# Order of transfers, of GpSimd's steps and of the work on normalized rows in a chain of attention layers

## The chip, the cores and the metric

The kernel runs on one core of a Trainium2 chip. The metric is the time of one execution on the device, in microseconds (us), the median of three. The core has five engines that run side by side: TensorE (matrix products), VectorE, ScalarE, GpSimd, and SyncE, which only issues transfers. Each takes its instructions in order; semaphores tie them together.

## The reference, cut to what matters

Eight batches of 512 tokens with 256 features go through eight stages. Five are attention with 16 heads of 16 features, two are two-layer networks, and the last is attention with heads of 64.

```
stage    kind
SELF0    x += attend(q, k, v of norm(x), causal) . W + b
CROSS0   x += attend(q of norm(x), k, v of ctx) . W + b
MLP0     x += gelu(norm(x) . W1 + b1) . W2 + b2
CROSS1   x += attend(q of norm(x), k, v of ctx) . W + b, weights quantized to -1, 0, 1 times a scale
SELF2    x += attend(q, k, v of norm(x), mask added) . W + b
CROSS2   as CROSS0
MLP2     as MLP0
SELF3    x += attend(q of norm(x), k, v of norm(ctx), causal) . W + b, heads of 64

attend:  scores = q . k^T * scale; softmax over keys (with the maximum of each query taken off); . v
```

## The kernel before

An attention stage is worked off in units: half a batch's heads, 8 heads x 512 queries x 512 keys, so 16 units of a stage (`UNITS`). Each engine runs the same sequence of slots, one for each unit, from `run_slots(engine, s, slot)`; `U` counts units over all stages, `u` those of a stage, `half` is `u % 2`. A stage whose predecessor is attention too is joined to it without a gap. In slot `u` TensorE works on three units at once:

- for unit u + 1, 32 tiles of maxima (`max_tile`: queries x keys, 128 queries x 512 keys, into the banks MX; VectorE reduces each to one maximum for a query),
- for unit u, 32 tiles of scores, turned (`score_tile`: keys x queries, into the banks ST; ScalarE takes the exponential into `prob`), and their products with the values (`values`, into OUT),
- for unit u + 2, the projections to keys and queries, and for each whole batch the values, the turning of the normalized rows (`T0`, `T1`) and the output projection (`O0`, `O1`). All of these pass through one bank L, one after the other: at which run of tiles each stands is written in the table `AT`, and `L_NO` numbers the uses of the bank. ScalarE or VectorE empties it and counts `l_free`; TensorE waits for that before the next use.

The maxima of a unit are needed as rows beside the stacked queries and keys. GpSimd splits them into a high and a low part (`split_max`), TensorE turns them (`M0` for the heads of group 0, `M1` for group 1), ScalarE copies them to `mrows` (`rows_out`), and SyncE copies two rows to `stk` (`max_rows`). Queries and keys are rounded to a high part `hi` and a remainder `lo` by GpSimd (`split`), and each of the two kinds (0 keys, 1 queries) is put into `stk` by three copies of 128 KB for each group of heads (`stack`), so that one matrix product holds all parts. At the first tile of a slot and at its 17th, TensorE waits for both kinds of stacked rows of that group of the next unit (`stack_in`) and for the rows of maxima of its own (`mrow_in`).

The other tasks of SyncE's queue in a slot: `move_few` and `move_raw` take the sums of exponentials and the raw products to other partitions, `spread_rows` and `widen` send the inverted sums through memory and back, `load_ctx` fetches a batch of the context. SyncE waits in order: whatever stands behind a wait waits too.

GpSimd multiplies the raw products by the inverted sums once for each unit (the operation at L1911, the scaling), and counts `at_ready`, for which the output projection O0 of an even slot waits. In CROSS1, whose weights are exact in the reduced format, the scaled products are also split in two parts (`output_parts`), and so are the normalized rows `hT` for the queries (`normed_parts`: `hT_hi`, then `hT_lo`), 14 times in attention slots; the first batch is done ahead of the stage. ScalarE writes `hT` out of bank L (`normalized`).

Of the kernel before, what the change touches and what calls it, by code (L numbers as in the profile page):

```python
# [73 lines left out]
def program(nc, x_in, ctx_in, ctx_rows_in, masks_in, shapes_in, cols_in, rows_in, wts, out):  # L74
# [12 lines left out]
    with es:  # L87
# [282 lines left out]
        def a_of(s, u, b):  # L370

            return (s + 1, b + 1 - NB) if isinstance(u, int) and u >= UNITS - 2 else (s, b + 1)
# [24 lines left out]
        def turn_of(s, u):  # L397

            if u == -2:
                return (s, 0) if s == SELF0 else None  # L400
            if u % 2 and (u + 1 < UNITS - 2 or s + 1 in JOINED and u < UNITS):
                return a_of(s, u + 1, (u + 1) // 2)
            return None
# [5 lines left out]
        L_NO = {}  # L409
# [118 lines left out]
        def _(sp):  # L528
# [25 lines left out]
            def attention(s):  # L554
                cross, causal, addmask = ATTN[s]
                n = ATTN_NO[s]

                def slot(u, c, b, p, on):
                    half, U, GB = c % 2, UNITS * n + u, NB * n + b
                    if u == 2:  # L560
                        load_next(s)
                    if (s, u) == (CROSS1, UNITS - 1):
                        sp.wait_ge(l_full, L_NO[s, u - 1, "O1"] + 1)
                        sp.dma_start(mask_k, masks_in[:, NT:2 * NT, :]).then_inc(masks_loaded, 16)
                    if on["stack1"]:
                        stack(U + 1, 1 - half, 1, 0)
                    if on["tail"]:
                        move_few(U - 1, 1 - half, 1)
                        move_raw(U - 1, 1 - half, 1, GB - 1 + half)
                    if on["b"]:  # L570
                        max_rows(U, half, 1)
                    if on["stack1"]:
                        stack(U + 1, 1 - half, 1, 1)
                    if on["tail"]:
                        spread_rows(U - 1, 1 - half)
                        widen(U - 1, 1 - half)
                    if cross and half == 0 and 0 <= b < NB - 2:
                        sp.wait_ge(l_full, L_NO[(*kq_slot(U + 1), "V1")] + 1)
                        load_ctx(b + 2, c // 2)
                    if on["a"]:  # L580
                        for kind in range(2):
                            stack(U + 2, half, 0, kind)
                    if on["b"]:
                        move_few(U, half, 0)
                    if on["m"]:
                        max_rows(U + 1, 1 - half, 0)
                    if on["b"]:
                        move_raw(U, half, 0, GB)

                def stack(U, half, g, kind):  # L590

                    if kind == 0:
                        wait(sp, st_full, 32 * (U - 2) + 16 * (g + 1))
                    sp.wait_ge(lo_done, 2 * U + kind + 1)
                    at = (8 if kind == 0 else 0) + G * g
                    for r, part in enumerate(((hi, lo, hi), (hi, hi, lo))[kind]):
                        lo_p = 64 * half + HD * r
                        sp.dma_start(stk[lo_p:lo_p + HD, at:at + G, :].bitcast(F32),
                                     part[64 * g:64 * g + 64, kind, :].bitcast(F32)).then_inc(stack_in[g][kind], 16)

                def max_rows(U, half, g):
                    sp.wait_ge(l_free, max_job(U, g) + 1)
                    lo_p = 64 * half + 3 * HD
                    sp.dma_start(stk[lo_p:lo_p + 2, G * g:G * g + G, :].bitcast(F32),
                                 mrows[32 * g:32 * g + 2 * G, :]).then_inc(mrow_in[g], 16)

                def move_few(U, half, g):

                    waits(sp, (ov_evac, 2 * U + g + 1),
                          (spread_out, 16 * (U - 1)))  # L610
                    sp.dma_start(few[64 * g:64 * g + 64, half, :], ovs[1:P:32, g, :].rearrange("h (c n) -> h c n", n=32)).then_inc(few_in[g], 16)

                def move_raw(U, half, g, GBu):

                    wait(sp, at_ready, BASE + U - 1)
                    if GBu > 0:
                        sp.wait_ge(l_full, out_job(GBu - 1) + 1)
                    sp.dma_start(raw[64 * g:64 * g + 64, half, :], ovs[0:P:2, g, :]).then_inc(raw_in[g], 16)

                def spread_rows(U, half):  # L620

                    sp.wait_ge(recip_done, U + 1)
                    sp.dma_start(spread[half].rearrange("h (c n) -> (h c) n", n=32), few[:, half, :]).then_inc(spread_out, 16)

                def widen(U, half):
                    waits(sp, (spread_out, 16 * (U + 1)), (at_ready, BASE + U))
                    rows = spread[half].rearrange("h (a n) -> h a n", a=1).broadcast_to([2 * G, HD, S])
                    sp.dma_start(sums[:, half, :], rows).then_inc(spread_in, 16)

                if cross and s not in JOINED:  # L630
                    load_ctx(1, 1)

                def with_stack1(u, c, b, p, on):
                    slot(u, c, b, p, dict(on, stack1=on["m"]))

                run_slots(sp, s, with_stack1)
# [544 lines left out]
        def _(act):  # L1181
# [5 lines left out]
            def attention(s):  # L1187
# [3 lines left out]
                def slot(u, c, b, p, on):  # L1191
                    half, U = c % 2, UNITS * n + u
                    sa, _ = a_of(s, u, b)
                    if u == -2 and not turned_ahead(s, u):
                        normalized(sa, u, 0)
                    if turned_ahead(s, u):
                        high_part(sa, u, U, half, 1)
                    place = AT[addmask]
                    for r, run in enumerate(RUNS[addmask]):
# [10 lines left out]
                        if on["b"] and r == FIRST_OUT[addmask]:  # L1210
                            product_out(U, 0)
                        if half == 0 and on["a"] and r == place["T1"] and not turned_ahead(s, u):
                            normalized(sa, u, 1)
                        if on["b"] and r == place["M1"]:
                            rows_out(u, U, 1)
                        if on["a"] and r in (place["K1"], place["Q"]) and not (turned_ahead(s, u) and r == place["Q"]):
# [1 line left out]
                        if on["m"] and r == place["M0"]:  # L1218
                            rows_out(u, U + 1, 0)
                        if half == 1 and r == place["T0"] and turn_of(s, u) is not None:  # L1220
                            normalized(turn_of(s, u)[0], u, 0)
                        for part in range(2):
                            if to_mlp(s, u, UNITS - 1) and r == place[f"K{part}"]:
                                first_turned(u, U, part)

                def normalized(sa, u, c):

                    job = L_NO[s, u, ("T0", "T1")[c]]
                    act.wait_ge(l_full, job + 1)
                    nc.scalar.activation(hT[:, c, :], L[:, :], ACT.Identity, **scale_shift(sa, c)).then_inc(l_free, 1)  # L1230

                def first_turned(u, U, c):
# [185 lines left out]
        def _(dve):  # L1418
# [34 lines left out]
            def invert(U, half):  # L1453
# [2 lines left out]
                    dve.wait_ge(few_in[g], 16 * U)  # L1456
                nc.vector.reciprocal(few[:, half, :], few[:, half, :]).then_inc(recip_done, 1)

            def low_normed(c):
                nc.vector.tensor_tensor(lo[:, c, :], hT[:, c, :], hi[:, c, :].bitcast(F32), ALU.subtract).then_inc(ml_lo, 1)  # L1460

            def attention(s):
# [3 lines left out]
                def slot(u, c, b, p, on):  # L1466
# [13 lines left out]
                    for r, run in enumerate(RUNS[addmask]):  # L1480
                        for k in run:
                            if on["m"] and k % 16 == 0:
                                wait(dve, max_split, 2 * (U + 1) - 3 + k // 16)
                            if on["m"]:
                                max_tile(m_of(s, u), U + 1, 1 - half, k)
                            if on["b"] and addmask and k % G in BY_VECTOR:
                                add_mask(u, U, k)
                        if u != -2 and norm is not None and r < 2:
                            sn, bn = norm
                            if r == 0 and (s, u) == (SELF0, -1):  # L1490
                                dve.wait_ge(x_loaded, 16)
                            if r == 0 and sn > 0:
                                wait(dve, x_done, NB * (sn - 1) + bn + 1)
                            for t in (2 * r, 2 * r + 1):
                                statistics(NB * sn + bn, xt(bn, t), t)
# [285 lines left out]
        def _(pool):  # L1781
# [56 lines left out]
            def attention(s):  # L1838
# [12 lines left out]
                def slot(u, c, b, p, on):  # L1851
# [10 lines left out]
                        clear(U - 1, 7)  # L1862
                    if on["b"]:
                        maxima(U, half, 1)
                    if s == CROSS1 and u >= 0 and half == 0 and on["a"] and a_of(s, u, b)[0] == s:
                        for kind, job in enumerate((L_NO[s, u - 1, "T0"], L_NO[s, u, "T1"])):
                            pool.wait_ge(l_free, job + 1)
                            normed_parts(b + 1, kind)
                    if clears:
                        clear(U, 0)  # L1870
                    if adds:
# [31 lines left out]
                        clear(U, 4)  # L1903
                    if adds:
                        add_mask(u, U, 4)
                    if on["tail"]:
                        for g in range(2):
                            pool.wait_ge(raw_in[g], 16 * U)
# [3 lines left out]
                                                ALU.mult).then_inc(raw_scaled if into_parts else at_ready, 1)  # L1912
                        if into_parts:
                            output_parts(UNITS - 1 if u == 0 else u - 1)
                    if on["a"]:
                        split(u, U, half, 1)
                    if clears:
                        clear(U, 5)
                    if adds:
# [268 lines left out]
```

## Time and profile before

| | |
|---|---|
| median of 3 runs | 3846.8 us |
| lowest and highest | 3839.29 and 3864.33 us |
| profiled execution | 3851.18 us |
| its span, first to last instruction | 3849.1 us |
| granted TensorE clock, mean | 0.963 of 2.4 GHz |
| busy: TensorE, VectorE, ScalarE, GpSimd | 3607.1, 2775.6, 2455.8, 2132.5 us |

Busy times are sums over stages of different kinds, so the stretches of the single stages say more than they do. The attention stages with heads of 16 take these stretches of the span: SELF0 about 66 to 500 us, CROSS0 to 922, CROSS1 1210 to 1653, SELF2 to 2220, CROSS2 to 2646. A slot lasts 25 to 30 us in SELF0, 28 in CROSS0 and CROSS2, 27 in CROSS1 and 33 to 38 in SELF2.

### The profile page before, as it was taken

The page shows a single profiled execution, that of the slowest core. Times are in us where ns is not written, and L with a number is a line of the kernel's source. Part 1 is how long each engine was busy: PE and PEld are TensorE (multiplying, and loading weights), DVE is VectorE, ACT ScalarE, POOL GpSimd, SP SyncE. Part 2 cuts the span into 40 slices and gives each one's busy share as a digit, 9 for nine tenths or more (in the row PEclk, how much of TensorE's full clock was granted, in tenths as well). Part 3 has the DMA queues.
Part 4 walks back from the last instruction along what each step waited for, and adds up shares of the span by engine and source line. Part 5 has one row for each costly group of instructions (what it writes and reads, how often), then busy time and mean ns, then how long its engine had stood idle before and what let it go on. Part 6 is the DMA issues. An engine that isn't in the chain of part 4 may idle for free.

```text
span 3849.1 us, 69127 instructions
## 1 busy us (share of the span) xinstructions
PE 3607.1 (94%) x21778; PEld 2053.1 (53%) x21778; DVE 2775.6 (72%) x6841; ACT 2455.8 (64%) x5254; POOL 2132.5 (55%) x2103
## 2 busy tenths in 40 slices
PE   6999999999998999999999999999899999999998
PEld 3444444444884444333333344444787777776776
DVE  4566677776676788789999878776766666666664
ACT  2555567777333777778888877776236666666664
POOL 3465544332344555378988843422436767776765
PEclk8999999999997999989999999998899999999998
DMA  4433344432003534333222243431100000000000
GB/s 109 100 83 81 85 107 86 86 84 50 20 1 67 112 86 95 86 74 76 60 61 67 59 107 85 91 83 41 46 6 6 12 12 7 12 12 7 12 7 6
DMA packets 135374, 220.50 MB, mean 57 GB/s; under 512 B 42721, under 2 KB 44641, under 8 KB 133217
## 3 DMA queue, kind: packets, MB, share of 16 engines
q1 hardware_dynamic: 135008, 216.02, 25.0%
q8 instruction: 182, 2.98, 0.4%
q14 instruction: 184, 1.50, 0.2%
HBM read 59.69 MB, written 5.51 MB: 17 GB/s over the span
## 4 chain that ended last, share of the span: by engine, by line
PE 58%; DVE 16%; POOL 11%; ACT 5%; issue 5%; DMA 3%; SPq 1%; DVEq 0%; POOLq 0%; ACTq 0%
PE MX L703 17%; PE L L703 14%; PE OUT L703 12%; PE ST L703 11%; DVE mx L1523 4%; POOL prob L1968 3%; DVE h_lo L1566 2%; DVE h_hi L1564 2%; POOL prob L2040 2%; ACT prob L1262 2%; DVE MX L1516 1%; PE L L928 1%; PE MX L1069 1%; POOL lo L1958 1%; DMA stk<-mrows 1%
## 5 line engine op out<-in xcount | busy, mean ns | idle before, releaser
L1262 ACT ACTIVATE prob<-ST 128x512 f32<-128x512 f32 (+3 forms) x2304 | 1149.8, 572 | 428.2 <-PE ST L703 423.2
L1523 DVE TENSOR_REDUCE mx<-MX 128x1 f32<-128x512 f32 x1536 | 961.8, 682 | 199.0 <-PE MX L703 198.2
L703 PE MATMUL MX<-stk 48*128 48x512 f32 (+3 forms) x2560 | 913.6, 444 | 92.8 <-DMA stk<-lo 27.8
L703 PE MATMUL ST<-stk 50*128 50x512 f32 (+3 forms) x2560 | 934.4, 446 | 5.6 <-ACT prob L1262 4.2
L703 PEld LDWEIGHTS MX<-stk 48*128 48x128 f32 x2560 | 424.4, 191 | 678.5 <-DVE mx L1523 277.8
L2040 POOL TENSOR_SCALAR prob<-prob,mx 128x128 f32<-128x128 f32 (+3 forms) x512 | 557.2, 1101 | 278.9 <-DVE mx L1714 278.9
L703 PE MATMUL OUT<-prob,V 128*32 128x512 f32 (+3 forms) x5120 | 667.9, 595 | 10.7 <-ACT prob L1272 6.0
L703 PEld LDWEIGHTS ST<-stk 50*128 50x128 f32 x2560 | 428.0, 189 | 56.6 <-ACT prob L1262 23.5
L1516 DVE CUSTOM_DVE_ANT_0 MX<-MX,W_even 128x512 f32<-128x512 f32 x512 | 347.2, 700 | 40.0 <-PE MX L703 39.7
L1968 POOL TENSOR_TENSOR prob<-prob,W_odd 128x512 f32<-128x512 f32 x256 | 324.0, 1282 | 76.0 <-ACT prob L1262 75.5
L1520 DVE CUSTOM_DVE_ANT_0 MX<-MX,later 128x128 f32<-128x128 f32 (+3 forms) x512 | 237.2, 518 | 129.3 <-PE MX L703 128.4
L1272 ACT ACTIVATE prob<-prob 128x512 f32<-128x512 f32 x512 | 304.9, 624 | 12.1 <-POOL prob L1968 11.7
L1811 POOL TENSOR_TENSOR X<-X,brow 128x1024 f32<-128x1024 f32 x56 | 135.9, 2426 | 249.8 <-DVE X L1442 249.8
L1722 DVE COPY PT<-MX 128x128 f32<-128x128 f32 (+3 forms) x256 | 124.9, 488 | 196.3 <-PE MX L1069 196.3
L1355 ACT ACTIVATE prob<-MX,mx 128x128 f32<-128x128 f32 (+3 forms) x256 | 135.3, 528 | 136.2 <-DVE mx L1708 134.5
L703 PEld LDWEIGHTS OUT<-prob,V 128*32 128x32 f32 x5120 | 102.1, 109 | 220.5 <-issue 194.1
L1956 POOL CAST hi<-Pr 128x512 fp32r<-128x512 f32 x160 | 97.6, 610 | 219.2 <-ACT Pr L1249 199.2
L1958 POOL TENSOR_TENSOR lo<-Pr,hi 128x512 fp32r<-128x512 f32 x160 | 204.5, 1278 | 12.9
L1302 ACT ACTIVATE V<-MX,cols 128x512 f32<-128x512 f32 x64 | 44.0, 690 | 231.5 <-PE MX L703 231.5
L1975 POOL TENSOR_SCALAR_AFFINE_SELECT prob<-prob 128x512 f32<-128x512 f32 x128 | 81.3, 635 | 185.0 <-ACT prob L1262 185.0
L1532 DVE TENSOR_TENSOR prob<-ST,W_odd 128x512 f32<-128x512 f32 x256 | 175.2, 684 | 0.0
L1249 ACT ACTIVATE Pr<-L,cols 128x512 f32<-128x512 f32 x128 | 88.0, 688 | 136.4 <-PE L L703 133.7
(238 smaller groups left out, 7527.8 us busy)
## 6 DMA issues: line engine op xcount, KB each, us to landing
stk<-hi SPq DMA_DIRECT2D x640, 128.0 KB, 3.8
stk<-lo SPq DMA_DIRECT2D x320, 128.0 KB, 3.9
misc<-misc SPq DMA_DIRECT2D x160, 128.0 KB, 2.8
sums<-spread SPq DMA_DIRECT2D x80, 256.0 KB
ctx_full<-in_ctx_t SPq DMA_DIRECT2D x24, 512.0 KB, 6.9
W_even<-in_w SPq DMA_DIRECT2D x2, 2048.0 KB, 11.3
XH<-in_ctx_rows SPq DMA_DIRECT2D x8, 512.0 KB, 3.6
X<-in_x_t SPq DMA_DIRECT2D x1, 3584.0 KB, 14.7
```

The costliest lines, as they stand in the source:

```text
L703: return nc.tensor.matmul(o, l, r, start=start, stop=stop)
L1262: nc.scalar.activation(prob_at(k)[:, q0:S], STB[k % RING][:, q0:S], ACT.Copy if addmask else ACT.Exp).then_inc(ex_done, 2 if addmask else 1)
L1272: nc.scalar.activation(tile, tile, ACT.Exp).then_inc(late_done, 1)
L1355: nc.scalar.activation(P3(qt, h)[:, 0:k_n], S3[h][t % 2][:, 0:k_n], ACT.Exp, bias=low3[:, qt, h:h + 1], scale=-1.0, accum_out=total3[:, qt ...
L1516: nc.vector.tensor_tensor_reduce(bank[:, :], bank[:, :], mask_q[:, qt, :], 1.0, -3.0e38, ALU.add, ALU.max, m).then_inc(mx_red, 1)
L1520: nc.vector.tensor_tensor_reduce(bank[:, 0:k_n], bank[:, 0:k_n], later0[:, S - k_n:S], 1.0, -3.0e38, ALU.add, ALU.max, m).then_inc(mx_red, 1)
L1523: nc.vector.tensor_reduce(m, bank[:, :], AX.X, ALU.max).then_inc(mx_red, 1)
L1532: nc.vector.tensor_tensor(prob_at(k), STB[k % RING], mask_k[:, i % 4, :], ALU.add).then_inc(st_masked, 1)
L1811: nc.gpsimd.tensor_tensor(xt(b, 0, NT), xt(b, 0, NT), bias, ALU.add).then_inc(x_done, 1)
L1958: nc.gpsimd.tensor_tensor(lo[:, kind, :], kq[:, kind, :], hi[:, kind, :].bitcast(F32), ALU.subtract).then_inc(lo_done, 1)
L1968: nc.gpsimd.tensor_tensor(tile, tile, mask_k[:, i % 4, :], ALU.add).then_inc(pool_masked, 1)
L2040: nc.gpsimd.tensor_scalar(tile, tile, inv3[:, qt, h:h + 1], None, ALU.mult).then_inc(nm3_done, 1)
```

## The change

In every attention stage, SyncE's copy of the rows of maxima for group 0 goes between the stacked keys and the stacked queries of that group, ahead of the queries and of `move_few`. In every attention stage, GpSimd splits the queries (kind 1) ahead of the scaling. In CROSS1, for all batches but the first, ScalarE writes the high part `hT_hi` itself, out of bank L and ahead of `hT`, and VectorE subtracts to get `hT_lo` in the second and third run of tiles of an even slot; GpSimd's `normed_parts` is left out there.

```diff
@@ SyncE, slot
                     if on["a"]:
-                        for kind in range(2):
-                            stack(U + 2, half, 0, kind)
+                        stack(U + 2, half, 0, 0)
+                    if on["m"]:
+                        max_rows(U + 1, 1 - half, 0)
+                    if on["a"]:
+                        stack(U + 2, half, 0, 1)
                     if on["b"]:
                         move_few(U, half, 0)
-                    if on["m"]:
-                        max_rows(U + 1, 1 - half, 0)
                     if on["b"]:
                         move_raw(U, half, 0, GB)
@@ ScalarE
-                def normalized(sa, u, c):
+                def normalized(sa, ba, u, c):
                     job = L_NO[s, u, ("T0", "T1")[c]]
                     act.wait_ge(l_full, job + 1)
+                    if sa == CROSS1:
+                        nc.scalar.activation(hT_hi[ba == 0][:, c, :], L[:, :], ACT.Identity, **scale_shift(sa, c)).then_inc(h_high, 1)
                     nc.scalar.activation(hT[:, c, :], L[:, :], ACT.Identity, **scale_shift(sa, c)).then_inc(l_free, 1)
@@ VectorE
+            def low_part(ba, c):
+                nc.vector.tensor_tensor(hT_lo[:, c, :], hT[:, c, :], hT_hi[ba == 0][:, c, :].bitcast(F32),
+                                        ALU.subtract).then_inc(h_low, 1)
...
+                        if half == 0 and u >= 0 and on["a"] and sa == CROSS1 and r in (1, 2):
+                            dve.wait_ge(l_free, L_NO[(s, u - 1, "T0") if r == 1 else (s, u, "T1")] + 1)
+                            low_part(b + 1, r - 1)
@@ GpSimd, slot
                     if on["b"]:
                         maxima(U, half, 1)
-                    if s == CROSS1 and u >= 0 and half == 0 and on["a"] and a_of(s, u, b)[0] == s:
-                        for kind, job in enumerate((L_NO[s, u - 1, "T0"], L_NO[s, u, "T1"])):
-                            pool.wait_ge(l_free, job + 1)
-                            normed_parts(b + 1, kind)
...
                     if adds:
                         add_mask(u, U, 4)
+                    if on["a"]:
+                        split(u, U, half, 1)
                     if on["tail"]:
                         for g in range(2):
                             pool.wait_ge(raw_in[g], 16 * U)
...
                             output_parts(UNITS - 1 if u == 0 else u - 1)
-                    if on["a"]:
-                        split(u, U, half, 1)
                     if clears:
                         clear(U, 5)
```

## Rows read from the trace of the kernel before

**Rows 1.** Windows: SELF0, CROSS0, CROSS1, SELF2: length, busy, clock, DMA share, GB/s

```profile
65.80:499.90 434.10, 411.58 (x2613) 205.60 (x2612) 283.37 (x1104) 248.78 (x623) 236.12 (x316) 0.95 0.39 85
499.90:922.50 422.60, 413.06 (x2530) 181.83 (x2529) 331.76 (x581) 305.47 (x582) 155.79 (x181) 1.00 0.42 89
1210.00:1653.00 443.00, 415.82 (x2601) 178.15 (x2600) 356.95 (x654) 332.61 (x624) 223.54 (x253) 0.98 0.42 92
1653.00:2220.30 567.30, 520.42 (x2631) 217.38 (x2629) 518.94 (x1361) 468.22 (x877) 481.29 (x448) 0.93 0.29 66
```

**Rows 2.** Waits of TensorE, total us, times, longest: CROSS1, then CROSS0

```profile
PE MX L703 <- DMA stk<-mrows: 18.4, 12, 2.5
...
PE MX L703 <- DVE mx L1523: 4.2, 17, 0.7
```

**Rows 3.** SyncE's queue in time, two slots of CROSS0: start us, us

```profile
704.86 0.70 SPq L604 DMA_DIRECT2D stk<-mrows  x1
...
706.86 0.60 SPq L598 DMA_DIRECT2D stk<-lo  x1
...
720.20 0.60 SPq L598 DMA_DIRECT2D stk<-lo  x1
...
722.75 0.68 SPq L604 DMA_DIRECT2D stk<-mrows  x1
```

**Rows 4.** ScalarE's rows and TensorE's next slot start: CROSS0 twice, SELF0, CROSS1 twice

```profile
722.14 0.59 ACT L1277 ACTIVATE mrows<-L 8x512 f32<-8x512 f32 x1 [0.32 <-PE L L928]
727.80 0.50 PE L703 MATMUL MX<-stk 48*128 48x512 f32 x1
...
692.77 0.59 ACT L1277 ACTIVATE mrows<-L 8x512 f32<-8x512 f32 x1 [0.69 <-PE L L928]
700.06 0.50 PE L703 MATMUL MX<-stk 48*128 48x512 f32 x1
...
334.58 0.59 ACT L1277 ACTIVATE mrows<-L 8x512 f32<-8x512 f32 x1 [0.82 <-PE L L928]
339.63 0.29 PE L703 MATMUL MX<-stk 48*128 48x128 f32 x1
...
1449.91 0.59 ACT L1277 ACTIVATE mrows<-L 8x512 f32<-8x512 f32 x1 [0.65 <-PE L L928]
1457.01 0.46 PE L703 MATMUL MX<-stk 48*128 48x512 f32 x1 [1.30 <-DMA stk<-mrows]
...
1232.31 0.59 ACT L1277 ACTIVATE mrows<-L 8x512 f32<-8x512 f32 x1 [0.65 <-PE L L928]
1235.75 0.49 PE L703 MATMUL MX<-stk 48*128 48x512 f32 x1
```

**Rows 5.** Transfers: KB, us from issue to landing; chain: landing to TensorE's start

```profile
stk<-lo SPq DMA_DIRECT2D x320, 128.0 KB, 3.9
...
570.93 0.09 issue
```

**Rows 6.** SELF2: GpSimd in time, TensorE, its waits for GpSimd, VectorE

```profile
1890.11 1.29 POOL L1911 TENSOR_TENSOR misc<-misc,sums 128x512 f32<-128x512 f32 x1
...
1892.03 1.27 POOL L1958 TENSOR_TENSOR lo<-Pr,hi 128x512 fp32r<-128x512 f32 x1
...
1891.45 0.48 PE L703 MATMUL L<-W_even,misc 128*128 128x256 f32 x1 [0.45 <-POOL misc L1911]
...
PE L L703 <- POOL misc L1911: 3.2, 7, 0.6
PE L L703 <- POOL raw_lo L1945: 2.5, 1, 2.5
...
1893.48 0.69 DVE L1442 TENSOR_TENSOR X<-L,X 128x512 f32<-128x512 f32 x1 [0.51 <-PE L L703]
```

**Rows 7.** CROSS1, an even slot in time: ScalarE, TensorE, GpSimd

```profile
1432.41 0.78 ACT L1230 ACTIVATE hT<-L,cols 128x512 f32<-128x512 f32 x1
...
1433.24 0.27 PE L928 MATMUL L<-ident,mhl 128*8 128x128 f32 x1
...
1440.42 0.61 POOL L1956 CAST hi<-Pr 128x512 fp32r<-128x512 f32 x1 [5.21 <-ACT Pr L1249]
```

More of the change, by code:

```diff
@@ L1194, in slot @@
                     if u == -2 and not turned_ahead(s, u):
-                        normalized(sa, u, 0)
+                        normalized(sa, 0, u, 0)
                     if turned_ahead(s, u):
@@ L1212, in slot @@
                         if half == 0 and on["a"] and r == place["T1"] and not turned_ahead(s, u):
-                            normalized(sa, u, 1)
+                            normalized(*a_of(s, u, b), u, 1)
                         if on["b"] and r == place["M1"]:
@@ L1220, in slot @@
                         if half == 1 and r == place["T0"] and turn_of(s, u) is not None:
-                            normalized(turn_of(s, u)[0], u, 0)
+                            normalized(*turn_of(s, u), u, 0)
                         for part in range(2):
```

## The prediction

> **What bounds the kernel now.** I call one of the 16 half-batches of an attention stage a slot; in a slot TensorE does 32 tiles of maxima of the next unit and 32 of scores of its own. I read the windows first, one for each attention stage [rows 1]. TensorE is busy 413 of 423 us in CROSS0, 416 of 443 in CROSS1, 412 of 434 in SELF0 and 520 of 567 in SELF2, while VectorE has 332, 357, 283 and 519. So TensorE's own queue sets the time, and a wait that ends in it is paid in full; in SELF2 VectorE is as tight, and no slack is left there either. Then I read who waits for whom on TensorE [rows 2]. In CROSS1 it waits 12 times, 18.4 us in all, for the rows of maxima to land: that is what the change is after. In CROSS0 no such wait is in the list at all; the list's longest is 4.2 us for VectorE.
>
> **Where the slot starts.** TensorE starts a slot when three things have landed for heads of group 0: stacked keys, stacked queries, and the rows of maxima. The last two are what the change swaps in SyncE's queue. In CROSS0 the queries went out long before (third copy issued at 720.20) and the queue then stood idle until ScalarE had the rows of maxima; it sent them at 722.75, at once [rows 3]. ScalarE finished them at 722.14 + 0.59 = 722.73, and TensorE went on at 727.80 without a wait [rows 4]: 5.07 us later. That is the time in which anything issued behind the rows has to land. After an even slot it is 700.06 - 693.36 = 6.70 us; in SELF0 before an even slot 339.63 - 335.17 = 4.46 us; in CROSS1 1457.01 - 1450.50 = 6.51 us, of which 1.30 are the wait [rows 4].
>
> **The swap in SyncE's queue.** After the change the three copies of queries stand behind the rows of maxima, and the rows wait for ScalarE. The same order is already used for the heads of group 1, so its price is in the trace: from the issue of rows of maxima to that of the third copy behind it 706.86 - 704.86 = 2.00 us [rows 3]. The third copy lands 3.9 us after its issue (the median of 320) [rows 5], and TensorE starts 0.09 us after a landing [rows 5]. With 0.02 from ScalarE's end to the issue, a slot can't start before ScalarE's end + 0.02 + 2.00 + 3.9 + 0.1 = 6.0 us. Against the distances above:
> CROSS0, starts of even slots: 6.0 - 5.07 = 0.95 us late, 7 of them (u = 2 to 14), 6.6 us. CROSS2 has the same code and the same work: 6.6 us. Starts of odd slots have 6.70 and lose nothing.
> SELF0, even: 6.0 - 4.46 = 1.55 us, 7 of them: 10.9 us.
> CROSS1 in its middle: the start moves from 6.5 (odd) to 6.0; before even slots the gain is some 0.2. About 12 starts, on average 0.35 us each: 4 us saved. This is all that is left of the 18.4 us, since the queries take the place of the rows as what lands last.
> CROSS1, u = 1: ScalarE ends at 1232.90 and TensorE starts at 1235.75 without a wait [rows 4], 2.85 us; it will be 6.0, so 3.1 us.
> The other first and last starts of the stages, some eight with distances between the ones shown: 0 to 12 us, I take 8 (about 1 each, as in CROSS0).
> SELF2: ScalarE has the rows ready far ahead there, the queries are last in either order; 0.
> The swap costs 6.6 + 6.6 + 10.9 - 4 + 3.1 + 8 = 31 us. The copies of sums of exponentials and of raw products move behind the queries too; they are read in the next slot, and cost nothing as long as the queue is empty by then: the rows and five more issues of 0.6 us each are out some 3.9 us after ScalarE's end, ahead of the slot's start.
> What is not shown is whether the three copies land as fast here as elsewhere: between 3.9 us alone for one copy after 2.00 us of issues, and nothing at all, if their first packets ran beside the rows. The row is of the same copies in the same order, so I take it.
>
> A rule of the Trainium skill speaks for less. The page "DMA: Bandwidth & Descriptors", section "Anatomy of one DMA — SWDGE (gpsimd) path", gives a copy about 2.0 us plus its bytes by 436 GB/s; 128 KB would be an estimated 2.3 us, and the queries would land 4.4 us after ScalarE's end, inside all distances but that of u = 1. The section is about copies that GpSimd issues, these are SyncE's, and the traced 3.9 us decides.
>
> **GpSimd's order.** The splitting of the queries (0.6 and 1.3 us) moves ahead of the scaling of the product. In the trace the scaling ends at 1891.39 and the splitting at 1893.30 [rows 6], so the scaling ends 1.91 us later from now on, and the queries 1.3 us earlier (3.2 in CROSS1, where the scaling also makes two parts). Earlier queries help nothing where SyncE holds them behind the rows. Later scaling costs where the output projection waits for it. That is SELF2: TensorE starts the projection at 1891.45, the moment the scaling is done, after 0.45 us of waiting; the stage has 7 such waits, and one more for the parts of CROSS1's last batch [rows 6]. So 8 x 1.91 = 15.3 us. VectorE, which could have hidden it, idles at the same place already, 0.51 us for that projection [rows 6], and finds no other work in its order. In CROSS0 and CROSS1 TensorE's list has no wait for the scaling [rows 2], and I take 0 there; with a margin of less than 1.9 us it would be up to 1 us for each of 16 projections. If TensorE caught up behind VectorE, SELF2 would pay 5 us; more than 15.3 has no mechanism.
>
> **Parts of rows in CROSS1.** GpSimd loses 14 pairs of operations, ScalarE gains 14 of 0.78 us and VectorE 14 of some 0.69. GpSimd stood idle 5.2 us before its splitting of keys [rows 7], so it didn't bound anything. ScalarE's new one stands between the transposed rows and the release of their bank, and TensorE's turning of the maxima needs that bank: it begins at 1433.24, just as ScalarE ends 1432.41 + 0.78 = 1433.19 [rows 7]. Every even slot moves by 0.75 us there, 7 of them: 5.2 us. The second bank of each batch is released at the end of an odd slot, a run of tiles ahead of its next use: 0. VectorE's 0.69 us fall into a stage where it is busy 357 of 443 us [rows 1], and are hidden by a ring of three banks; bounds 0 and 14 x 0.69 = 10 us.
> Here the Trainium skill has a warning: by "SBUF — State Buffer", section "Who interferes with whom", a VectorE operation with two inputs in SBUF and a GpSimd operation that reads SBUF lock each other out. GpSimd has no work at that point of the slot once its parts are gone, so the estimate by the rule is 0, and at worst one GpSimd operation of 1.3 us for each of the 14; no row here shows the two beside each other.
>
> **TensorE's clock.** It was granted fully in CROSS0 (1.00) and at 0.98 in CROSS1, which has the waits, 0.95 in SELF0 and 0.93 in SELF2 [rows 1]; these are means over stretches at 2.4 and at 1.2 GHz, so that 0.02 less is 2% of the time. If CROSS0 and CROSS2 fell to CROSS1's level, twice 423 us x 0.02 = 17 us; if the other two lost as much, 20 more. Below: 0. Rows of a stage with waits of this size are nearer to the small end, and I take 6.
>
> **Sum.** 31 + 15.3 + 5.2 + 6 = 58 us. The profiled execution took 3851.2 us (span 3849.1), 4.4 above the median of three, 3846.8. So 3909 on its own scale and 3905 on the median's: 1.5% slower.
>
> **Rivals.**
> (a) Not slower. The queries never land last: the decisive number is the time from ScalarE's end to their landing, 6.0 by my rows; at 4.4 or below no start but that of u = 1 is late, and CROSS1's 18.4 us are gained whole. For it: the trace shows no query copy in that place for group 0. Against it: the same three copies behind the same rows, group 1. 3847 - 18 + 15 + 5 = 3849; with SELF2's price gone as well, 3834. Chance 0.17, of which 0.05 is faster by over 1%: only with clock given back too.
> The estimate from the Trainium skill's "DMA: Bandwidth & Descriptors" would put the landing at those 4.4 us; the trace doesn't bear it out for any copy of this size.
> (b) SELF2 hides the later scaling, because TensorE is ahead of VectorE's maxima in most of the stage (it waits for them at slot starts). Against it is VectorE's own idle time at that place. 3905 - 10 to 15 = 3892. Chance 0.15.
> (c) The start waits are partly made good inside the slot, so that half of the 31 are paid: 3889. For it: TensorE's busy time is not its peak. Chance 0.10.
> (d) The clock falls in the wake of the new waits, most of the 37 us above: 3935 to 3950. For it: the two stages with most waits have the lowest clock. Chance 0.10.
> The forecast itself: 0.48.
>
> A measurement of this kernel tells about 1% from no change (the three runs spread over 0.65%), so slower means above 3885. The forecast, (b), (c) and (d) lie mostly above it, but (c) and part of (b) with a small clock term lie close: slower 0.70, same 0.25, faster 0.05. For 8 in 10 the range goes down into the upper part of (a), 3856, and up into (d), 3940.
>
> **What the new profile would show.** Right: TensorE's waits for maxima rows gone from CROSS1 and waits for the third query copy in their place, about 1 us at even starts of CROSS0 and CROSS2 and 1.5 in SELF0, ScalarE's end to slot start at 6.0; in SELF2 the wait for the scaling at 2.4 instead of 0.45; in CROSS1 a wait of 0.7 before the turned maxima. Wrong: slots of CROSS0 as long as before (the landing is shorter), or SELF2's slots as long (hidden). What would break the sum: another landing time of the copies, or clock stretches that move by tens of us.

## The result

The changed kernel takes 3927.0 us (median of 4, 3909.95 to 3945.51) against 3853.2 us for the kernel before (median of 4, 3839.29 to 3864.33). The ratio is 1.0194, with a 95% interval of 1.0133 to 1.0256: slower by some 74 us. The profiled execution took 3920.8 us, 69.6 more than that of before, and its span is 3919.0 us.

### The profile after

First the windows of the changed kernel, one for each attention stage: SELF0, CROSS0, CROSS1, SELF2, CROSS2. The columns are those of [rows 1]: length, then busy time and instructions of TensorE, its weight loads, VectorE, ScalarE and GpSimd, then the granted clock, the DMA share and GB/s.

```profile
68.70:525.40 456.70, 427.47 (x2614) 209.81 (x2614) 283.37 (x1102) 250.75 (x623) 236.23 (x316) 0.90 0.38 81
525.40:959.80 434.40, 415.89 (x2528) 181.75 (x2528) 331.67 (x580) 305.86 (x581) 156.01 (x178) 0.99 0.41 86
1248.20:1696.60 448.40, 417.49 (x2602) 179.95 (x2602) 365.43 (x668) 341.65 (x638) 197.40 (x224) 0.97 0.43 92
1696.60:2284.20 587.60, 526.12 (x2629) 219.97 (x2629) 520.27 (x1361) 468.92 (x877) 481.59 (x445) 0.92 0.29 64
2284.20:2719.70 435.50, 418.66 (x2535) 182.22 (x2535) 332.05 (x581) 309.16 (x586) 157.69 (x182) 0.99 0.41 86
```

CROSS2 in the kernel before, which [rows 1] leaves out:

```profile
2220.30:2646.00 425.70, 418.13 (x2536) 183.29 (x2536) 332.39 (x581) 308.18 (x586) 156.79 (x182) 0.99 0.41 88
```

TensorE has the same instructions in both kernels (the counts of a stage differ by two at most). So each stage's loss can be split in two: what its busy time grew by is time in which it ran slower, at the clock's lower level; what is left of the length (length less busy) is time in which it stood. From these windows and [rows 1]:

| stage | length | TensorE busy | TensorE standing |
|---|---|---|---|
| SELF0 | +22.6 | +15.9 | +6.7 |
| CROSS0 | +11.8 | +2.8 | +9.0 |
| CROSS1 | +5.4 | +1.7 | +3.7 |
| SELF2 | +20.3 | +5.7 | +14.6 |
| CROSS2 | +9.8 | +0.5 | +9.3 |
| sum | +69.9 | +26.6 | +43.3 |

The spans differ by the same 69.9 us (3919.0 - 3849.1): outside these stages the differences cancel (2.9 us more ahead of SELF0, 0.9 more between CROSS0 and CROSS1, 3.8 less behind CROSS2). Each kernel's column is one execution, and the clock differs from one execution to the next. How much the busy column can be trusted is seen in the traces of the experiments below. SELF0 was busy 401.0 to 416.8 us in seven traces without the swap there, and 427.5, 436.6 and 438.2 in the three with it, so its growth is real. SELF2 was busy 516.4 to 531.1 us in four traces in which the code of the stage was unchanged, so its +5.7 says nothing.

**What TensorE waits for.** TensorE's list of waits in CROSS0, then CROSS1, then SELF2 (total us, times, longest):

```profile
PE MX L704 <- issue: 8.4, 8, 1.6
...
PE MX L704 <- DMA stk<-lo: 3.0, 2, 2.0
```

```profile
PE MX L704 <- issue: 17.3, 15, 2.0
PE MX L704 <- DMA stk<-lo: 6.5, 3, 3.5
PE L L929 <- ACT hT L1233: 3.4, 6, 0.6
```

```profile
PE L L929 <- POOL mhl L1846: 21.0, 16, 2.8
PE L L704 <- POOL misc L1920: 16.5, 7, 2.4
...
PE L L704 <- POOL raw_lo L1952: 4.4, 1, 4.4
```

"Issue" says that the profile matched no releaser. The wait for `stk<-mrows` of [rows 2] is gone from CROSS1, but waits of these two kinds stand at the same starts: the twelve that took 18.4 us now take 15.4, and u = 1, which had none, waits 3.5. CROSS0 had two waits of these kinds, 2.1 us in all, and has ten. What ended them is seen by following one start of CROSS0 through three engines in time (start us, length us): ScalarE, SyncE's queue, TensorE.

```profile
753.46 0.59 ACT L1280 ACTIVATE mrows<-L 8x512 f32<-8x512 f32 x1 [0.32 <-PE L L929]
...
754.07 0.69 SPq L605 DMA_DIRECT2D stk<-mrows  x1
754.80 1.19 SPq L599 DMA_DIRECT2D stk<-hi  x2
756.04 0.60 SPq L599 DMA_DIRECT2D stk<-lo  x1
...
760.20 0.46 PE L704 MATMUL MX<-stk 48*128 48x512 f32 x1 [1.03 <-issue]
```

ScalarE ends at 754.05; the rows go out at once, the third copy of the queries at 756.04, 1.97 us behind; TensorE starts at 760.20. That is 6.15 us after ScalarE's end, where the distance was 5.07 before [rows 3, 4]. The third copy explains it: the median of all 320 from issue to landing is 3.9 us in this trace too, as in [rows 5], and 0.02 + 1.97 + 3.9 is 5.9 of the 6.15. The other even starts agree: 6.14 to 6.20 us from u = 2 to 12 in CROSS0 and 6.59 at u = 14; in SELF0 6.13 to 6.16 at five of the seven, 6.63 and 6.42 at the other two.

In SELF2 GpSimd now finishes the scaling at 1944.82 + 1.27 = 1946.09, behind the splitting; TensorE starts the projection at 1946.15, and VectorE, which had idled 0.51 us for it [rows 6], idles 2.42:

```profile
1943.59 1.28 POOL L1965 TENSOR_TENSOR lo<-Pr,hi 128x512 fp32r<-128x512 f32 x1
1944.82 1.27 POOL L1920 TENSOR_TENSOR misc<-misc,sums 128x512 f32<-128x512 f32 x1
...
1946.15 1.99 PE L704 MATMUL L<-W_even,misc 128*128 128x256 f32 x8 [2.35 <-POOL misc L1920]
...
1948.18 0.69 DVE L1445 TENSOR_TENSOR X<-L,X 128x512 f32<-128x512 f32 x1 [2.42 <-PE L L704]
```

**Where the clock fell.** One even start of SELF0 in the changed kernel: TensorE's first product, then windows of 6.7 us from there (TensorE's busy time comes first behind the length, the granted clock third from the end).

```profile
353.27 0.29 PE L704 MATMUL MX<-stk 48*128 48x128 f32 x1 [1.67 <-issue]
```

```profile
353.30:360.00 6.70, 6.70 (x38) 3.69 (x42) 3.44 (x15) 5.50 (x11) 0.64 (x1) 0.53 0.40 60
360.00:366.70 6.70, 6.70 (x32) 1.96 (x24) 2.68 (x12) 1.72 (x6) 1.27 (x2) 0.71 0.30 61
```

The same place of the kernel before, whose slot starts at 339.63 without a wait [rows 4]:

```profile
339.60:346.30 6.70, 5.98 (x45) 3.14 (x44) 4.37 (x20) 6.37 (x13) 1.47 (x5) 1.00 0.37 82
346.30:353.00 6.70, 6.67 (x41) 2.63 (x40) 4.50 (x19) 3.48 (x10) 2.34 (x5) 1.00 0.36 75
```

After a wait of 1.67 us TensorE runs the next ones at 0.53 and 0.71 of 2.4 GHz, which is mostly its lower level of 1.2 GHz; without the wait it keeps 1.00 there. In the changed kernel such a stretch of 7 to 10 us begins within 0.6 us of the start at all seven even slots u = 2 to 14 of SELF0, in the kernel before at none of them. Over the whole stage the clock's record has 92 us at the lower level in the changed kernel and 41 in the kernel before. So the theory for what the forecast undersized was: the swap's waits are as computed, and they cost the clock as well. The rival was that waits or transfers somewhere else had grown.

### The profile page after: what moved, and what is told of

Read it like the earlier page. It is cut to its first block, busy times and chain, and to the rows that moved or that the text cites. A ratio compares the mean times of both kernels' runs of the same rounds, so it can differ in the third digit from the quotient of the medians.

```text
span 3919.0 us, 69127 instructions
## 1 busy us (share of the span) xinstructions
PE 3629.8 (93%) x21778; PEld 2057.2 (52%) x21778; DVE 2782.2 (71%) x6855; ACT 2472.7 (63%) x5268; POOL 2110.7 (54%) x2075
## 4 chain that ended last, share of the span: by engine, by line
PE 61%; DVE 14%; POOL 11%; issue 6%; ACT 5%; DMA 2%; SPq 1%; DVEq 0%; POOLq 0%; ACTq 0%
PE MX L704 17%; PE L L704 15%; PE OUT L704 13%; PE ST L704 11%; DVE mx L1534 4%; POOL prob L1975 3%; DVE h_lo L1577 2%; DVE h_hi L1575 2%; POOL prob L2047 2%; DMA stk<-lo 2%; PE L L929 1%; PE L L727 1%; ACT prob L1265 1%; PE MX L1070 1%; DVE st L1426 1%
## 5 line engine op out<-in xcount | busy, mean ns | idle before, releaser
L704 PE MATMUL OUT<-prob,V 128*32 128x512 f32 (+3 forms) x5120 | 678.7, 604 | 7.8 <-POOL prob L1982 4.1
L1844 POOL CAST mhl<-mx 128x16 fp32r<-128x16 f32 x160 | 33.2, 207 | 263.7 <-DVE mx L1534 247.9
```

Source lines behind the costliest of these rows:

```text
L704: return nc.tensor.matmul(o, l, r, start=start, stop=stop)
```

## The experiments

Every time stands beside runs of the kernel before on the same chip; ratios are to those, with 95% intervals.

### The three parts alone

The swap in SyncE's queue alone, all stages:

```diff
                     if on["a"]:
-                        for kind in range(2):
-                            stack(U + 2, half, 0, kind)
-                    if on["b"]:
-                        move_few(U, half, 0)
+                        stack(U + 2, half, 0, 0)
                     if on["m"]:
                         max_rows(U + 1, 1 - half, 0)
+                    if on["a"]:
+                        stack(U + 2, half, 0, 1)
+                    if on["b"]:
+                        move_few(U, half, 0)
```

> The swap in SyncE's queue alone. Queue theory (queries that go out behind the rows of maxima land last, 6.1 us after ScalarE's end): 31 us slower by the prediction's sum, up to 40 with clock, most of it in SELF0, CROSS0 and CROSS2, about 1 us at each start of an even slot there; CROSS1 within 5 us of before. Rival (clock: the loss is in stretches at 1.2 GHz and not in the waits): well under 31 us, with CROSS0 as long as before.

Measured: 3918.9 us, ratio 1.0173 (1.0136 to 1.0209), some 67 us. The windows of SELF0, CROSS0 and CROSS2:

```profile
69.80:534.80 465.00, 436.59 (x2614) 213.52 (x2614) 283.76 (x1102) 252.37 (x624) 236.85 (x318) 0.88 0.38 80
534.80:969.50 434.70, 417.32 (x2528) 181.97 (x2528) 331.72 (x580) 305.83 (x581) 155.57 (x178) 0.99 0.41 86
...
2278.10:2718.40 440.30, 421.16 (x2535) 182.92 (x2535) 332.12 (x581) 309.93 (x589) 158.70 (x183) 0.98 0.41 85
```

Standing grew by 5.9, 7.8 and 11.6 us in these and by 3.2 in CROSS1 (30.4 for 27.2): 28.5 us, where I had computed 31. In SELF2 it didn't grow. Busy time grew by 25.0 us in SELF0 alone, by 4.3, 3.3 and 3.0 in CROSS0, CROSS1 and CROSS2, and fell by 2.7 in SELF2: 33 us in all. The other 11.7 us by which this span is longer than that of before (3922.3 for 3849.1) lie outside these stages, and no experiment shows why. So the waits were sized right and the clock was not: up to 40 us were expected and 67 measured. The swap is nearly the whole loss, and nearly half of its profiled loss is growth of busy time.

GpSimd's order alone, all stages:

```diff
+                    if on["a"]:
+                        split(u, U, half, 1)
                     if on["tail"]:
...
                             output_parts(UNITS - 1 if u == 0 else u - 1)
-                    if on["a"]:
-                        split(u, U, half, 1)
```

> GpSimd's order alone, in all stages. Own theory: SELF2 longer by 15 us (8 waits for the scaling, 1.9 us each more), CROSS1 shorter by up to 18 us, since the queries' copies leave 3 us earlier and the rows of maxima no longer queue behind them; the sum within 5 us of before. Rival (the order is free because VectorE bounds SELF2): 18 us faster than before.

Measured: 3853.6 us, 0.9984 (0.9959 to 1.0009): no change that can be measured. But it is two opposite effects, CROSS1 and SELF2 in the windows:

```profile
1221.90:1640.90 419.00, 410.70 (x2601) 177.95 (x2600) 356.56 (x654) 331.58 (x624) 223.97 (x253) 0.99 0.49 98
1640.90:2232.60 591.70, 531.13 (x2631) 221.03 (x2630) 522.40 (x1361) 469.94 (x877) 482.37 (x448) 0.90 0.28 63
```

CROSS1 is 24 us shorter than in [rows 1], SELF2 24 us longer.

The parts of rows by ScalarE and VectorE alone (the edits to `normalized`, `low_part` and `normed_parts` of the diff ahead of the prediction, with both orders as before):

> The parts of rows by ScalarE and VectorE alone. Own theory: a new wait of 0.5 to 0.75 us ahead of the turned maxima in 7 even slots of CROSS1, 0 to 5 us slower, partly absorbed by the wait for the rows of maxima that is still there. Rival (freeing GpSimd is what brings the gain): CROSS1 shorter by 5 us or more.

Measured: 3862.6 us, 1.0013 (0.9991 to 1.0034). In CROSS1 TensorE's waits for ScalarE ahead of the turned maxima are there, and the waits for rows of maxima of [rows 2] stay:

```profile
PE MX L703 <- DMA stk<-mrows: 19.1, 12, 2.5
PE L L928 <- ACT hT L1232: 4.4, 7, 0.6
```

4.4 us for the computed 5.2: right. The stage's standing grew by 4.1 us (31.3 for 27.2).

### GpSimd's order, stage by stage

The same edit with the condition `s == CROSS1`, and with `s == SELF2`:

```diff
+                    if on["a"] and (s == CROSS1):
+                        split(u, U, half, 1)
                     if on["tail"]:
...
-                    if on["a"]:
+                    if on["a"] and not (s == CROSS1):
                         split(u, U, half, 1)
```

> GpSimd's order in CROSS1 only, everything else as before. Own theory: all of the 12 waits for rows of maxima go and nothing takes their place, because the queries leave some 3 us before the rows are ready: 18 us faster, 0.5%. Rival (another wait ends at the same place, as with the swap): within 5 us of before.

> GpSimd's order in SELF2 only. Own theory: 8 waits for the scaling 1.9 us longer each, 15 us slower, plus some us of lower clock (24 us more in SELF2 with the order in all stages). Rival (VectorE's backlog hides them): within 5 us of before.

Measured: in CROSS1 alone 3830.6 us, 0.9942 (0.9923 to 0.9961), 22 us faster than the kernel before and by its ratio the fastest of all versions. In SELF2 alone 3882.8 us, 1.0054 (1.0034 to 1.0074), 21 us slower: in its trace the stage is 29.6 us longer (596.9), with 15.7 us more standing, where 15.3 were computed, and 13.9 more busy time, some of which the unchanged stage shows in other traces too. The two cancel, as the run with both shows.

Why CROSS1 gains is seen in SyncE's queue. GpSimd in the kernel before (scaling, its parts, then the queries' parts), and the queue:

```profile
1445.88 1.27 POOL L1911 TENSOR_TENSOR misc<-misc,sums 128x512 f32<-128x512 f32 x1 [2.77 <-DMA sums<-spread]
...
1449.83 1.28 POOL L1958 TENSOR_TENSOR lo<-Pr,hi 128x512 fp32r<-128x512 f32 x1
...
1443.94 8.39 SPq L598 DMA_DIRECT2D stk<-hi  x3
1452.37 0.60 SPq L598 DMA_DIRECT2D stk<-lo  x1
...
1453.71 0.68 SPq L604 DMA_DIRECT2D stk<-mrows  x1
```

The rows were ready at 1450.50 [rows 4] and went out at 1453.71: they stood behind the queries' copies, these waited for GpSimd, and GpSimd had stood 2.77 us for the inverted sums. With the queries' parts first:

```profile
1447.11 1.28 POOL L1960 TENSOR_TENSOR lo<-Pr,hi 128x512 fp32r<-128x512 f32 x1
1448.36 1.27 POOL L1913 TENSOR_TENSOR misc<-misc,sums 128x512 f32<-128x512 f32 x1
...
1449.65 0.60 SPq L598 DMA_DIRECT2D stk<-lo  x1
...
1451.88 0.59 ACT L1277 ACTIVATE mrows<-L 8x512 f32<-8x512 f32 x1 [0.64 <-PE L L928]
...
1452.49 0.68 SPq L604 DMA_DIRECT2D stk<-mrows  x1
...
1457.61 0.50 PE L703 MATMUL MX<-stk 48*128 48x512 f32 x1
```

The queue is empty when ScalarE ends (1452.47), the rows go out at 1452.49, and TensorE starts 5.14 us after ScalarE's end instead of 6.51, without a wait. No wait for the rows is left in this stage, and it is 20.8 us shorter than before (422.2 for 443.0), 18.3 of them standing. In the change itself the swap puts the queries behind the rows and takes this gain away again.

For SELF2 the gain to be had would be to move the scaling ahead instead. I took the fastest version and let GpSimd do the scaling between its two additions of the mask in even slots:

```diff
+                    early = adds and half == 0
                     if adds:
-                        add_mask(u, U, 4)
+                        add_mask(u, U, 4, BY_POOL[:1] if early else BY_POOL)
...
+                        if early:
+                            add_mask(u, U, 4, BY_POOL[1:])
```

> GpSimd's order in CROSS1 only, and the opposite move in SELF2: in even slots the scaling goes 1.3 us earlier, between the two mask additions ahead of it. Own theory (TensorE's wait for the scaling is paid in full): those waits, 5.7 us in all before, go, and SELF2 is some 5 us shorter; in all 20 to 25 us faster than before. Rival (the later mask addition holds up its exponential instead): no faster than the order in CROSS1 alone, with TensorE's waits for ScalarE's exponentials longer.

Measured: 3836.7 us, 0.9949 (0.993 to 0.9968): 20 us faster than the kernel before, but not faster than the order in CROSS1 alone. The wait for the scaling is gone from SELF2's list. TensorE stands 40.8 us there, instead of 43.4 with the order in CROSS1 alone and 46.9 in the kernel before, but it is busy 531.7 us instead of 521.9 and 520.4, at a clock of 0.90:

```profile
1647.10:2219.60 572.50, 531.73 (x2630) 219.89 (x2629) 519.86 (x1361) 470.70 (x877) 481.34 (x447) 0.90 0.29 66
```

What was saved in waits didn't show in the time. The rival's reason isn't seen: TensorE's waits for exponentials ahead of its products with the values are 2.1 us, against 2.0 with the order in CROSS1 alone. Whether the edit itself lowers the clock isn't settled: with the code of this stage unchanged it lasted from 562.9 to 573.7 us over the experiments.

### The swap, stage by stage

In SyncE's slot `ahead = s == CROSS0`, and the rows go ahead of the queries where `ahead` is true, else as before; then the same with `s == SELF0`.

```diff
+                    ahead = s == CROSS0
...
+                        stack(U + 2, half, 0, 0)
+                    if on["m"] and ahead:
+                        max_rows(U + 1, 1 - half, 0)
+                    if on["a"]:
+                        stack(U + 2, half, 0, 1)
...
-                    if on["m"]:
+                    if on["m"] and not ahead:
```

> The swap in CROSS0 only. Own theory: starts of even slots 1.0 to 1.1 us later, 8 of them, 9 to 12 us slower in all, without more than 10 us at the lower clock, since the waits there are shorter. Rival (the clock follows any such wait): 20 us slower.

> The swap in SyncE's queue in SELF0 only. Wait theory (the swap costs the waits it makes): 12 to 15 us slower. Clock theory (each wait of some 1.6 us at the start of an even slot is followed by 7 to 10 us at 1.2 GHz, as in both traces with the swap): SELF0 25 us or more longer, with 50 us more at the lower clock than before.

Measured: CROSS0 alone 3868.9 us, 1.0024 (1.0008 to 1.004), some 9 us; SELF0 alone 3893.2 us, 1.0083 (1.0055 to 1.011), some 32 us. Seven even starts, late by about 1 us each, cost CROSS0 what the waits are: TensorE's standing there grew by 9.4 us and its busy time by 5.4. In SELF0 waits of 1.7 us at the starts cost three times my 10.9, and the clock's record has 116 us at the lower level for the 41 of before, as the clock theory wanted. Its windows, whole and after an even start:

```profile
68.60:535.60 467.00, 438.21 (x2614) 213.49 (x2614) 283.12 (x1102) 251.25 (x623) 235.99 (x316) 0.88 0.38 79
...
359.90:366.60 6.70, 6.70 (x38) 3.75 (x42) 3.40 (x15) 5.46 (x11) 0.63 (x1) 0.53 0.40 60
```

To see whether the low clock comes from standing, I filled these waits: the swap in SELF0, and TensorE works off twelve 128 x 128 products with the identity ahead of its wait in even slots. They write a bank that the first tile overwrites.

```diff
+                            if k == 0 and on["m"] and s == SELF0 and half == 0:
+                                wait(pe, mx_red, TILES * U + before(0) + 1)
+                                for _ in range(12):
+                                    mm(MXB[0][:, 0:P], identr[:, :], identr[:, :])
```

> The same swap in SELF0, and TensorE does 12 small products of the identity (about 1.3 us, written to a bank that the next tile overwrites) ahead of its wait at the start of each even slot of SELF0. They compute nothing that is used. The queries still land 6.1 us after ScalarE's end, so the slot can't start sooner. Clock theory: no long stretches at 1.2 GHz after these starts, 8 to 15 us faster than with the swap in SELF0 alone. Wait theory: the same time as that, or slower if the products take longer than the wait.

Measured: 3886.7 us, 1.0069 (1.0049 to 1.009): 6 us less than unfilled, but the intervals overlap. The same start, and the windows after it:

```profile
357.73 1.53 PE L707 MATMUL MX<-identr 128*128 128x128 f32 x12
359.64 0.29 PE L707 MATMUL MX<-stk 48*128 48x128 f32 x1 [0.37 <-issue]
```

```profile
359.60:366.30 6.70, 5.97 (x44) 3.05 (x44) 4.16 (x18) 5.71 (x12) 1.16 (x2) 1.00 0.39 59
366.30:373.00 6.70, 6.53 (x40) 2.63 (x40) 4.50 (x19) 3.49 (x10) 2.34 (x5) 1.00 0.35 74
```

The start is as late as without them, 6.15 us after ScalarE's end in both, and the clock stays at 1.00 in these two windows. So it is with all the filled starts of the stage: no low stretch begins there. Standing, not lateness, brings the low stretch. Low stretches elsewhere in the stage stay (72 us in all, against 116 unfilled and 41 before); one begins 14 to 18 us after each of the seven starts.

Over the stage TensorE's busy time without the fillers (10.8 us) falls from 438.2 to 431.8 - 10.8 = 421.0 us. Of these 17.2 us only 7.9 are gained in the stage (467.0 to 459.1), because other waits come back: those for `hT`, 5.2 us before and none in the swapped kernels, are 4.8 us again, and one for VectorE takes 2.7. A slower TensorE had been hiding those for `hT`. So in this stage the clock's cost is less than the growth of busy time. In the whole time the filled kernel's gain is too small for these runs, and the two profiled executions (3897.5 and 3900.4 us) don't show it at all.

### The parts together

GpSimd's order in all stages and the parts of rows, without the swap; and the fastest version with the parts of rows added:

> The changed kernel with SyncE's queue as it was before: GpSimd's order in all stages and the parts of rows. Own theory: the swap is what costs; CROSS1 some 15 us shorter than before, SELF2 15 to 25 us longer, within 15 us of the kernel before in all and 55 us or more faster than the changed kernel. Rival (the three parts need each other, and the loss comes from order or parts): still 30 us or more slower than before.

> GpSimd's order in CROSS1 only, with the parts of rows by ScalarE and VectorE. Own theory: the waits for rows of maxima are gone already with the order, so the parts only add 3 to 5 us of waits ahead of the turned maxima: 13 to 15 us faster than before, 3 to 5 us slower than with the order alone. Rival (GpSimd's free time helps once the rows don't wait): 5 us or more faster than the order alone.

Measured: all but the swap 3866.8 us, 1.0032 (1.0015 to 1.005), so the swap costs 1.0194 / 1.0032 = 1.016 on top of the rest, as it does alone. The rival is out, but one step of the expectation is too: CROSS1 lasted 439.5 us, 3.5 shorter than before and not 15, at 424.9 busy and a clock of 0.96. The order in CROSS1 with the parts of rows 3850.5 us, 0.9991 (0.997 to 1.0011): 0.0049, 19 us, slower than the order alone, where some 5 us of waits were expected. The wait, and the window of CROSS1 in this kernel:

```profile
PE L L928 <- ACT hT L1232: 8.5, 7, 1.3
```

```profile
1200.20:1638.90 438.70, 424.02 (x2603) 181.19 (x2602) 365.59 (x668) 340.69 (x638) 197.31 (x225) 0.96 0.46 93
```

and the window of CROSS1 with the order alone:

```profile
1221.20:1643.40 422.20, 413.29 (x2601) 178.35 (x2600) 356.58 (x654) 331.64 (x624) 223.56 (x253) 0.98 0.48 97
```

Once the start waits are gone, the wait for ScalarE grows from 0.6 to 1.2 us each. ScalarE used to catch up while TensorE stood at the start. Now it is late: TensorE has filled the bank at 1309.70 + 0.66 = 1310.36, and ScalarE begins on it 0.80 us later, behind three exponentials and a copy of the products:

```profile
1309.70 0.66 PE L726 MATMUL L<-ident,XH 128*128 128x128 f32 x4
...
1311.16 0.81 ACT L1231 ACTIVATE hT_hi_later<-L,cols 128x512 fp32r<-128x512 f32 x1
```

With the parts alone it began 0.03 us after, at a start with a wait of 1.16 us (1383.27 for 1383.24). Standing grows by 14.7 - 8.9 = 5.8 us, busy time by 10.7: again more busy time is added than standing. The low stretches stand where the new wait is: one of 3.4 to 6.8 us begins within 1.5 us of five of the six waits of 1.33 us. The kernel with all but the swap shows it at five of six too, within 2.3 us. This makes the parts of rows dear just where the order made the stage fast.

## Why the prediction was right, and where its terms were not

The forecast was 3905 us, 1.015 of its median before; the interval of the measured ratio, 1.0194 (1.0133 to 1.0256), includes that. The waits came where they were said to come and at nearly their size. One term, the clock's, was far too small, and the total is closer than its terms because the waits were put somewhat too high: that part is luck.

**Slot start at ScalarE's end + 6.0.** Right, a little short: 6.15 in CROSS0, 353.27 - (346.52 + 0.59) = 6.16 in SELF0, where ScalarE's row is

```profile
346.52 0.59 ACT L1280 ACTIVATE mrows<-L 8x512 f32<-8x512 f32 x1 [0.81 <-PE L L929]
```

The row of the same copies in another place of the slot was a good price. Rival (a), the queries never last, is out. The estimate of 2.3 us for 128 KB by the rule of the Trainium skill's "DMA: Bandwidth & Descriptors", section "Anatomy of one DMA — SWDGE (gpsimd) path", doesn't hold for these copies: from SyncE's queue they took 3.9 us. The rule is for copies that GpSimd issues, and no run here tests it on those. The nearest copy of this size in SyncE's queue, `misc<-misc`, had a median of 2.8 us in the trace of before, so the landing time goes by the kind of copy too, and the row of the same copies was the one to take.

**The swap's waits, 31 us.** 28.5 in the swap alone, as growth of TensorE's standing. In CROSS1 the twelve waits fell by 3.0 us for the computed 4, and u = 1 waits 3.5 for 3.1. CROSS0 and CROSS2 took 9.0 and 9.3 in the changed kernel for 6.6 and their edges. SELF0 took 6.7 net for 10.9 and its edges, since its waits for `hT` vanished meanwhile.

**SELF2, 15.3 us.** 14.6 of standing, 15.7 with the order in SELF2 alone. Waits for the scaling grew from 3.2 to 16.5 and from 2.5 to 4.4 us. Rival (b), hidden in part, is out; TensorE's wait for the maxima's parts even grew from 17.0 to 21.0 us, which I hadn't computed, while its waits for VectorE fell.

**Parts of rows, 5.2 us.** 3.4 in the changed kernel (6 waits of 0.6), 4.4 alone. The rule of the Trainium skill's "SBUF — State Buffer", section "Who interferes with whom", was not put to the test: none of VectorE's 14 subtractions in CROSS1 (0.68 us each) ran at the same time as an instruction of GpSimd, neither in the changed kernel nor in the order in CROSS1 with the parts of rows. That GpSimd has no work at that point, as the prediction had it, was right.

**The clock, 6 us: mis-sized.** This is the step that failed. TensorE's busy time grew by 26.6 us, 15.9 of them in SELF0. Standing was computed at 52 us and came to 43.3, so the sum of 58 against 69.6 hides two errors: some 8 us too much in waits and 20 too little for the clock. I had reasoned from stages' mean clocks that CROSS1, with waits like the new ones, had lost only 0.02. That row was of the wrong stage, and of its 21.9 us at the lower level 8 were the end of a stretch that had begun in the stage before. The same table had SELF0 with VectorE, ScalarE and TensorE all less busy than in CROSS0, at 0.95. There each even start, with a wait of 1.6 to 2.1 us, was followed by 7 to 10 us at 1.2 GHz; in CROSS0 none of the six starts with a wait of 1.0 us was, and the stage's busy time grew by only 2.8 us. Rival (d), most of 37 us, was nearer to this term than my 6, though its total of 3935 to 3950 was not reached; (c), waits made good in the slot, holds only where SELF0's `hT` waits vanished.

**What I called worth nothing.** "Earlier queries help nothing where SyncE holds them behind the rows" holds for the change as a whole, and hid the better question: without the swap they free the queue for the rows. The 18.4 us of CROSS1 were to be had from GpSimd's order, not from SyncE's.

What stays open: why the waits of 0.8 to 3.5 us at the starts of CROSS1 in the changed kernel bring a low stretch at four of 15 only, of 3.4 us each (clock 0.97), while 1.33 us in the middle of an even slot brings one at five of six (0.96), so that the length of a wait alone doesn't decide; what moves SELF2's clock between executions and versions; and what filling SELF0's waits is worth in time.

## What to carry to other kernels

Where a transfer stands in a queue behind one that isn't ready, look first at why that one is late: here the engine that makes its data had other work in front, and moving that work in one stage gained 22 us, while reordering the queue in all stages lost 67. An order that is shared by stages has to be priced in each, since 24 us gained in one and 24 lost in another look like nothing. A new wait of TensorE is to be priced with the clock behind it, which needs rows of the same stage: split a stage's loss into TensorE's growth of busy time and of standing. The first overstates what the clock costs, since a slower TensorE waits less elsewhere: in SELF0 17.2 us less of it shortened the stage by 7.9.

## What the runs showed of the hardware

A wait of 1.67 us in SELF0 was followed by 13.4 us at a mean clock of 0.62 (windows of 0.53 and 0.71), and with twelve products of 1.53 us in all put into that wait it stayed at 1.00 for as long; waits of 1.0 us in CROSS0 were followed by none. Of three copies of 128 KB issued in a row by SyncE behind one of 16 KB the third landed 4.1 us after its issue (756.04 to 760.20 less 0.09), hardly more than the median of the same copy over all its places, 3.9. And a slower clock hides waits: SELF0's 5.2 us for `hT` vanished when it fell and were 4.8 again when the waits were filled, so the busy time that it adds is not all added to the stage.
